# Cross attention and a routed feed-forward layer on one core: head-turns, running sums and the end of attention placed elsewhere

## The reference, cut to what matters

```python
q = l2norm(latents @ Wq) * q_scale            # latents = layer_norm(layernorm(x))
k, v = split(concat([ctx, latents]) @ Wkv)    # k = l2norm(k) * k_scale
sim = einsum('bhid,bhjd->bhij', q, k) * 8
sim = where(full_mask, sim, -max)
attn = softmax(sim)                            # over 64 + 1024 keys
out = einsum('bhij,bhjd->bhid', attn, v)
x = x + layer_norm(out @ Wo)
xf = layernorm(x)
x = x + shared_swiglu(xf) + top2_of_16_experts(xf)
```

## Time and profile before

| | |
|---|---|
| median of 3 runs | 820.85 us (819.99 to 821.29) |
| the profiled execution | 821.29 us, of which its span is 819.6 us |
| TensorE busy | 796.2 us (97%) |
| VectorE, ScalarE, GpSimd busy | 500.8, 342.8, 361.2 us |
| attention's eight pairs | from about 111 to 476 us |
| granted TensorE clock, mean | 0.996 |

### The profile page before, as it was taken

The page is one execution under the profiler, slowest core; times in us unless marked ns, Lnnn a source line. Parts: engine busy times, 40 slices in busy tenths (PEclk is TensorE's granted clock), DMA queues, the critical chain, the costliest instruction groups (busy, mean ns, idle before and its releaser), DMA issues.

```text
span 819.6 us, 13057 instructions
## 1 busy us (share of the span) xinstructions
PE 796.2 (97%) x4375; PEld 485.5 (59%) x4376; DVE 500.8 (61%) x918; ACT 342.8 (42%) x645; POOL 361.2 (44%) x259
## 2 busy tenths in 40 slices
PE   7999999999999999999999979999999999999997
PEld 4444455555554555455544446766557999999654
DVE  3888767778686878687787376647212334333254
ACT  3545465565655666565665311121111333333110
POOL 2100035868586785868588932301661000000374
PEclk9999999999999999999999989999999999999999
DMA  4014700000000000000020011591522222222243
GB/s 117 27 39 157 261 1 1 1 27 1 27 2 27 1 27 2 3 26 1 27 65 27 14 53 38 160 333 54 186 90 70 91 90 90 90 90 90 78 144 107
DMA packets 52373, 55.99 MB, mean 68 GB/s; under 512 B 8922, under 2 KB 47460, under 8 KB 52324
## 3 DMA queue, kind: packets, MB, share of 16 engines
q1 hardware_dynamic: 49236, 46.96, 18.0%
q0 software_dynamic: 3072, 8.39, 3.1%
q10 hardware_dynamic: 16, 0.00, 0.0%
HBM read 36.60 MB, written 18.67 MB: 67 GB/s over the span
## 4 chain that ended last, share of the span: by engine, by line
PE 88%; issue 4%; POOL 3%; ACT 2%; DVE 2%; DVEq 0%; DMA 0%; POOLq 0%; SPq 0%; ACTq 0%
PE bank L1109 14%; PE bank L925 12%; PE bank L950 11%; PE bank L1172 10%; PE bank L798 10%; PE bank L1124 7%; PE bank L884 6%; PE bank L1181 5%; PE bank L930 4%; PE bank L1016 2%; PE bank L868 2%; POOL acc L698 2%; PE bank L1162 1%; ACT prob L1288 1%; PE bank L945 1%
## 5 line engine op out<-in xcount | busy, mean ns | idle before, releaser
L1498 DVE TENSOR_REDUCE mx<-bank 128x1 f32<-128x512 f32 x256 | 164.4, 686 | 46.3 <-PE bank L884 45.1
L1288 ACT ACTIVATE prob<-bank,zero 128x512 f32<-128x512 f32 x256 | 161.0, 684 | 74.7 <-PE bank L930 72.2
L698 POOL TENSOR_TENSOR acc<-acc,prob 128x1024 f32<-128x1024 f32 (+1 forms) x72 | 179.3, 2491 | 10.3
L950 PE MATMUL bank<-prob,vn 128*64 128x512 f32 x512 | 121.1, 602 | 0.0
L1109 PE MATMUL bank<-xfT,w12s 128*128 128x512 f32 x256 | 117.6, 605 | 0.8 <-ACT xfT L1345 0.8
L760 POOL DMA_INDIRECT slot_result<-slot_results,posi x32 | 31.2, 973 | 160.1 <-DMA slot_results<-yo 148.2
L690 POOL TENSOR_TENSOR acc<-prob 128x1024 f32<-128x1024 f32 x16 | 41.1, 2566 | 119.8 <-ACT prob L1288 98.2
L1172 PE MATMUL bank<-xsT,w_slot 128*128 128x128 f32 x752 | 91.9, 275 | 1.0 <-ACT xsT L1379 1.0
L1172 PEld LDWEIGHTS bank<-xsT,w_slot 128*128 128x128 f32 x752 | 89.2, 192 | 6.0 <-ACT xsT L1379 1.6
L1109 PEld LDWEIGHTS bank<-xfT,w12s 128*128 128x128 f32 x256 | 49.5, 194 | 51.5 <-issue 50.2
L1369 ACT ACTIVATE hidden_units<-bank 128x512 f32<-128x512 f32 x32 | 19.1, 597 | 132.9 <-PE bank L1109 132.9
(11 more groups left out here) (172 smaller groups left out, 1123.5 us busy)
## 6 DMA issues: line engine op xcount, KB each, us to landing
w12r<-in_L_ffn_routed_w SPq DMA_DIRECT2D x32, 256.0 KB, 4.2
slot_rows<-zrow SPq DMA_DIRECT2D x47, 128.0 KB, 1.9
xsl<-slot_rows SPq DMA_DIRECT2D x47, 128.0 KB, 2.0
slot_results<-yo SPq DMA_DIRECT2D x47, 128.0 KB, 1.7
w3r<-in_L_ffn_routed_w SPq DMA_DIRECT2D x16, 256.0 KB, 3.5
rec<-row_sum_reciprocals SPq DMA_DIRECT2D x28, 128.0 KB, 2.9
xin<-in_x SPq DMA_DIRECT2D x16, 128.0 KB, 2.0
w12s<-in_L_ffn_shared_w SPq DMA_DIRECT2D x2, 1024.0 KB, 6.6
```

The source lines that it names most:

```text
L698: g.tensor_tensor(acc[rows, c, :, :], acc[rows, c, :, :], prob[rows, n % PROBS, :, :], ALU.add).then_inc(summed, 1)
L950: last = mm_(o_bank(i, c)[rows, :], vn[:, kt, b, (2 * j + h) * DH:(2 * j + h + 1) * DH], prob[:, n % PROBS, h, :], start=(s == 0), stop=(s ...
L1288: a(prob[rows, held % PROBS, h, :], bank[2 * (n % 2) + h][rows, :], ACT.Exp, bias=bias[rows, :])\
L1498: v.tensor_reduce(mx[:, h, t, c:c + 1], ring_bank(u)[:, :], AX.X, ALU.max).then_inc(ring_used, 1)
```

## The change

1. Turns go to the head of phases 1, 2 and 4 (K_LEFT; Q_LEFT; K_RIGHT and K_CTX), ahead of the rounds of that position. The rounds of phases 1 to 5 move by a position or so: phase 3 now has round 0 at its head, none ahead of the second slot, and rounds 2 and 4 behind.
2. VectorE's additions move: `add_two` of tiles 6 and 7 from the end of phase 2 to the end of phase 3, `add_both` from inside phase 3 to the head of phase 4, `add_two` of tiles 15 and 16 from the end of phase 5 to the end of the next pair's phase 0. `invert_sums` moves to the end of phase 2, `divide` to the ends of phases 3 and 5.
3. `total_pair` goes from behind phase 0 to phase 1, ahead of its value products.
4. GpSimd takes `tail` of the left half later (`ADDED`), and in the last pair earlier (`LAST_ADDED`), with the bias additions ahead of that pair.
5. In the last pair the left sum comes behind phase 3, `project_o(0)` behind phase 4, `project_o(1)` behind phase 5. The right sum goes through ScalarE, `spread`, a 128x8 inversion and DRAM.

```diff
-LEFT_SUMMED, SUMS = 8, 13
+LEFT_SUMMED, SUMS = 11, 13
+LAST_LEFT_SUMMED = 6
...
-    NEXT_TURNS = {(1, 3): (K_LEFT,), (3, 0): (Q_LEFT,), (3, 3): (K_RIGHT, K_CTX)}
-    OWN_ROUNDS = {0: ((), (8,), (9,), (10,)), 1: ((11,), (12,), (13,), ()), 2: ((14,), (15,), (RIGHT_MASKED,), ())}
-    NEXT_ROUNDS = {3: ((), (0,), (2,), ()), 4: ((4,), (6,), (1,), (3,)), 5: ((5,), (7,), (LEFT_MASKED,), ())}
+    NEXT_TURNS = {(1, 0): (K_LEFT,), (2, 0): (Q_LEFT,), (4, 0): (K_RIGHT, K_CTX)}
+    OWN_ROUNDS = {0: ((), (8,), (9,), (10,)), 1: ((), (11,), (12,), (13,)), 2: ((), (14,), (15,), (RIGHT_MASKED,))}
+    NEXT_ROUNDS = {3: ((0,), (), (2,), (4,)), 4: ((), (6,), (1,), (3,)), 5: ((5,), (), (7,), (LEFT_MASKED,))}
...
+            sp.wait_ge(sum_kept, PAIRS)
+            sp.wait_ge(rec_ready, PAIRS - 1)
+            for rows in (LOW, HIGH):
+                sp.dma_start(spread[rows, 0:LAST_COLS], rec[rows.start:rows.start + 1, 0, :]
+                             .rearrange("a (p c) -> a p c", c=LAST_COLS)).then_inc(sum_spread, 16)
+            sp.wait_ge(rec_ready, PAIRS)
+            sp.dma_start(rec_dram[1, 0:2 * QC].rearrange("(p c) -> p c", p=P), spread_rec[:, 0:LAST_COLS])\
+                .then_inc(rec_stored, 16)
...
             if i == PAIRS - 1:
-                pool.wait_ge(c_loaded, 48)
-                add_bias(0)
-                add_bias(1)
+                add_last(i, 0, LEFT_TAIL, LAST_LEFT_SUMMED)
             add_first(i, 1, BOTH + 1)
             add_more(i, 1, BOTH, HIGH)
-            add_last(i, 0, LEFT_TAIL, LEFT_SUMMED)
-            for s in range(BOTH + 3, BOTH + 7):
+            for s in range(BOTH + 3, BOTH + 6):
                 add_more(i, 1, s)
+            if i < PAIRS - 1:
+                add_last(i, 0, LEFT_TAIL, LEFT_SUMMED)
+            add_more(i, 1, BOTH + 6)
+            if i == PAIRS - 1:
+                deviations_c(0)
             add_last(i, 1, TAILS, SUMS)
...
+                if f == 1 and i:
+                    total_pair(i - 1)
                 for one in weighed:
                     weigh(*one)
-                if f == 0 and i:
-                    total_pair(i - 1)
-                if not more and f == 4:
+                if not more and f == 3:
                     total(NCH - 2)
-            if not more:
-                project_o(0)
+                if not more and f > 3:
+                    project_o(f - 4)
...
+                if f == 4 and more:
+                    v.drain()
+                    add_both(i)
                 for a in range(len(slots) + 1):
-                    if f == 1 and a == BATCH and i:
-                        invert_sums(i - 1)
-                    if f == 3 and a == BATCH:
-                        v.drain()
-                        add_both(i)
-                        if i:
-                            divide(2 * i - 2)
...
+                if f == 0 and i:
+                    add_two(i - 1, BOTH + 7, left_summed(i - 1))
                 if f == 2:
                     negate(1)
+                    if i:
+                        invert_sums(i - 1)
+                if f == 3:
+                    if more and i:
+                        divide(2 * i - 2)
                     add_two(i, 6, 0)
...
+                if f == 5 and more:
+                    negate(0)
+                    if i:
+                        divide(2 * i - 1)
```

More of the change, by code:

```diff
@@ L349, in build @@
             for a in range(len(slots) + 1):
+                for turn in place_turns(i, f, a):
+                    ring_put("turn", *turn)
                 for j, r in place_rounds(i, f, a):
                     ring_rounds(j, (r,))
-                for turn in place_turns(i, f, a):
-                    ring_put("turn", *turn)
+            if f == 1 and i:
+                ring_put("sums", i - 1)
             if BOTH in WEIGHED[f]:
                 ring_put("o", i)
-            if f == 0 and i:
-                ring_put("sums", i - 1)
-            if i == PAIRS - 1 and f == 4:
-                ring_put("sum", NCH - 2)
+    ring_put("sum", NCH - 2)
     ring_put("y", 0)
@@ L554, in _, with spread_last @@
         repeat_rec(PAIRS - 2)
+        def spread_last():
+            sp.wait_ge(sum_kept, PAIRS)
[6 more added lines that the diff above has]
+                .then_inc(rec_stored, 16)
+            sp.wait_ge(rec_stored, 16 * PAIRS)
+            for h, rows in enumerate((LOW, HIGH)):
+                sp.dma_start(rec[rows, 1, :], rec_dram[1:2, h * QC:(h + 1) * QC].to_broadcast([DH, QC]))\
+                    .then_inc(rec_loaded, 16)
         w3_rows = sw3[0].rearrange("(u p) d -> p u d", p=P)
@@ L706, in _ @@
         for i in range(PAIRS):
+            if i == PAIRS - 1:
+                pool.wait_ge(c_loaded, 48)
+                add_bias(0)
+                add_bias(1)
             if i:
@@ L737, in _ @@
         g.drain().then_inc(d_consts, 1)
-        for t in range(2, TQ):
+        for t in range(EARLY + 1, TQ):
             deviations_c(t)
@@ L1013, in project_o @@
                 pe.wait_ge(y_used, t)
+            if t == EARLY + 1:
+                pe.wait_ge(sum_kept, PAIRS)
             for c in range(B):
@@ L1326, in stage_b @@
                     keep_o(i - 1, 1)
+                if f == 2 and i:
                     keep_sums(i - 1)
@@ L1337, in _ @@
             stage_b(i)
+        u = ring_at[("sum", NCH - 1)]
+        act.wait_ge(ring_made, made_to(u))
+        act.wait_ge(o_ready, NCH - 1)
+        a(rec[:, 0, :], ring_bank(u)[:, :], ACT.Copy).then_inc(sum_kept, 1)
         def copy_xfT(t):
@@ L1558, in invert_sums, with invert_last @@
             v.reciprocal(spread_rec[:, :], spread[:, :]).then_inc(rec_ready, 1)
+        def invert_last():
+            dve.wait_ge(sum_spread, 64 * (PAIRS - 1) + 32)
+            dve.wait_ge(rec_stored, 16 * (PAIRS - 1))
+            v.reciprocal(spread_rec[:, 0:LAST_COLS], spread[:, 0:LAST_COLS]).then_inc(rec_ready, 1)
         sum_squares(NT - 1, 1, True, 2 * (NT - 1))
@@ L1652, in _ @@
         stage_c(0)
+        add_two(PAIRS - 1, BOTH + 7, LAST_LEFT_SUMMED)
         stage_c(1)
+        invert_last()
+        stage_c(EARLY)
         divide(NCH - 1)
         v.drain()
-        stage_c(EARLY)
         hid = 0
```

56 lines of the change are left out of this document (33 added, 23 removed).

## The result

The changed kernel takes 882.21 us (median of 4 runs, 881.05 to 884.88) where the kernel before takes 820.88 us beside it: ratio 1.075, 95% interval 1.073 to 1.0771. It is **slower by 61 us**; 888 us was predicted. The profiled execution has a span of 883.2 us, 63.6 us above the one before, where the sum said 67.6.

A forecast was written before the change was run, and what follows sets the result against it. With TensorE 97% busy, only its queue's order and small waits were taken to matter. Terms -5.4 + 7 + 2.1 + 48.2 + 21.7 - 6 = +67.6 us on 819.6 gave 887.2; forecast 888 us, first three cases 826 to 893.

The forecast's parts named there:

- The additions at the pair's head: Pair heads: moving `add_two` of tiles 15 and 16 removes a 0.9 us wait in six pairs, -5.4 us.
- The rounds: Phases 0 to 5: two rounds and two masked ones leave ScalarE's floor, +1.0 us a pair, +7 us.
- the sums inside phase 1: Phase 1: sums right behind round 13 wait 0.3 us for a bank still being reduced, +2.1 us over seven.
- The border: Phases 3 to 4: TensorE idles until K_RIGHT's split, 7.3 us in six pairs, 4.4 in pair 0, +48.2 us.
- The strict alternation: Border of phases 3 and 4: GpSimd and VectorE take turns on the shared port; likeliest case, 888 us, chance 0.42.
- the reciprocals: Border of phases 3 and 4: loaded for `divide` at +2.1 us, counted from round 4 at position 3 of phase 3.
- TensorE's clock: After each of seven border waits the granted clock falls to its lower level, 3.1 us lost each, +21.7 us.
- The end: Behind attention: 4.11 us idle before `xf`'s second turn and 3.1 us low clock go, new waits come, -6 us.
- the way over DRAM: Last sums' inversion, 6.2 us and some, lies beside the third projection and the first shared units.
- one turn kept: Rival, border: VectorE keeps the port for the instruction right behind, 4.95 us a pair, 854 to 875 us, chance 0.25.
- no collision: Border, lower end: VectorE never meets GpSimd, wait 0.9 us a pair, 826 us; in the rival of chance 0.15.

The follow-up runs named there:

- experiment 6: The kernel before with only the addition of tiles 15 and 16 moved behind the next pair's phase 0 head, joint sums a phase on: 816.92 us, ratio 0.9944.
- experiment 10: experiment 8 with `divide` one round up, directly behind `add_both`: 828.43 us, ratio 1.0093.
- experiment 5: experiment 1 with `add_both` also put back, ahead of the round at position 3 of phase 3: 837.81 us, ratio 1.0192.
- experiment 1: The changed kernel with `add_two` of tiles 6 and 7 back behind phase 2's negated maxima, except in the last pair: 864.7 us, ratio 1.0481.
- experiment 2: The changed kernel with GpSimd's right-half additions narrowed from 512 to 8 columns a head in all pairs but the last: 837.29 us in one run.
- experiment 3: The changed kernel with VectorE's two border additions narrowed from 512 to 8 columns a head in all pairs but the last: 850.19 us in one run.
- experiment 4: The changed kernel with the load of the fourth residual tile ahead of `spread_last` on SyncE's queue: 881.08 us, ratio 1.0678.
- experiment 8: experiment 5 with `invert_sums` ahead of phase 2's last slot instead of behind `negate(1)`: 840.88 us, ratio 1.0202.
- the joined version: The kernel before's phases, rounds and border additions, with the change's head addition, sums and end, and SyncE's order of experiment 4: 812.17 us, ratio 0.9879.

## Why the prediction came out as it did

The runs form a ladder, read from the first to the last turned maxima: kernel before 333.0 us, experiment 6 327.6, experiment 10 338.4, experiment 5 348.0, experiment 1 372.0, the change 392.3. They come from different chips; phases 0 to 2 take 23.4 us in all that have the changed tables (experiments 1, 5, 10 and the change), so this step can be read across them.

- **The additions at the pair's head, -5.4 us.** Right in place and size: 333.0 to 327.6 us is -5.4 us (experiment 6).
- **The rounds, and the sums inside phase 1, +7 and +2.1 us.** Nearly right: 327.6 to 338.4 us is 10.8 us, of which 2.5 us are the wait of 0.42 us left in six pairs; the other 8.3 us stand where 9.1 were taken. This step holds all of the placement of turns and rounds; which part of it is whose wasn't tried apart.
- **The border, +48.2 us.** Right in mechanism, and shown from both sides by experiments 2 and 3. The waits sum to 45.2 us: 4.04 us in pair 0, where 4.4 were taken, and some 6.85 us in the six others, where 7.3 were. The strict alternation held in all seven pairs; each turn costs what is left of GpSimd's instruction and then VectorE's own. That VectorE might keep the port once didn't happen at this border. One step of it held by a narrow margin: the reciprocals, taken at +2.1 us, landed up to +3.9 us, just ahead of the end of GpSimd's first instruction. A few tenths later, as in one pair of experiment 4, the order breaks and the wait is 5.17 us.
- **A link the prediction missed.** The division also holds ScalarE's copy, and through it `k_hi` (experiment 5). In the changed kernel this lies beside the longer wait: ScalarE's `k_hi` starts at 298.47 there, 6 us ahead of `k_lo`. It surfaces when the additions are gone, and cost experiments 5 and 8 their 9.6 and 9.0 us over experiment 10, one fall of the clock in each included.
- **TensorE's clock, +21.7 us.** The falls came, seven of them, but this term was sized too large. The change lies 53.9 us above experiment 10 (392.3 - 338.4), which has 0.42 us of wait left in six pairs; with 45.2 us of waits, 11.2 us are left (53.9 + 2.5 - 45.2) for all seven falls and anything else, 1.6 us each instead of 3.1. Pair by pair it is 0.9 to 2.2 us. The price was read from a stretch in which TensorE worked 6.05 of 6.83 us. Here the fall begins inside the wait itself: of 302.49 to 309.32, TensorE works only 4.05 us, and half of that is what a clock of 0.50 can cost, about 2 us.
- **The end, -6 us.** This step failed in sign. The wait of 4.11 us before the second turn of `xf` is gone, as said, though one of 3.20 us stands at a later turn, and from the last turned maxima to the end it is 380.0 us instead of 375.4, +4.6 us. The new waits for the two sums were 0.65 us (at 510.53) and 2.22 us, where 1 and 1.9 us were taken. A wait of 1.23 us that it didn't have stands before the projection at 518.03. What the prediction left out most is who stands behind SyncE's new work. In its queue, then GpSimd's and TensorE's timelines:

```profile
538.12 1.13 SPq L570 DMA_DIRECT2D spread<-rec  x2
541.39 0.33 SPq L573 DMA_DIRECT2D row_sum_reciprocals<-spread_rec  x1
542.85 1.10 SPq L577 DMA_DIRECT2D rec<-row_sum_reciprocals  x2
543.99 1.06 SPq L559 DMA_DIRECT2D xres<-in_x  x2
...
548.45 1.26 POOL L703 TENSOR_TENSOR xres<-xres,lno 128x512 f32<-128x512 f32 x1 [7.97 <-DMA xres<-in_x]
...
550.81 0.88 DVE L1696 SCALAR_TENSOR_TENSOR x<-yn,rs,xres 128x256 f32<-128x256 f32 x2 [7.53 <-POOL rs L668]
...
556.18 1.13 PE L1157 MATMUL bank<-w3s,hidden_units 128*128 128x256 f32 x4 [2.80 <-DVE hidden_units L1674]
...
569.56 0.69 PE L1094 MATMUL bank<-ident,xf 128*128 128x128 f32 x2 [3.20 <-DVE xf L1460]
```

  `spread_last` holds SyncE from 538.12 to 543.9, the load of the residual tiles goes out at 543.99, and GpSimd waits 7.97 us for it with the bias addition, behind which the deviations of the next tiles stand. VectorE gets them at 550.81, and TensorE loses 2.80 and then 3.20 us, the second with a fall of the clock at 568.70. The prediction put the way over DRAM beside the third projection and costed it at nothing, by its data alone; it named no instruction behind it on the queue. Experiment 4 shows this: with the load moved ahead, both waits go and the end takes 375.2 us, 4.8 us less, and that with the late wait of 2.67 us in it. In the joined version it takes 372.2 us, so of the 6 us that were predicted 3.2 us can be had.

The total came close by luck in this: two terms erred in opposite ways, the end by +10.6 us, and the clock by some -10 (11.2 instead of 21.7). The large term, 48.2 for 45.2 us, came out of its own mechanism. Two of the rivals' times don't follow from the prediction's own terms: one turn kept adds up to 852.7 us and not 854, and no collision to 825 us and not 826. Nothing hangs on either. The Trainium skill, in "SBUF — State Buffer", section "SBUF: two separate sides", has whichever instruction starts first take the shared port pair for its length; the rows above agree, each VectorE addition ending 1.08 us behind a GpSimd instruction that had begun ahead of it. In experiment 10 VectorE starts 0.36 us ahead and isn't slowed.

## What to carry to other kernels

Before moving VectorE work with two SBUF inputs into a gap, count how many such instructions in a row would meet a GpSimd that always has more: each pays the rest of a GpSimd instruction (some 2 us here), whatever its own size, and what matters is the instruction that stands behind them. The same work placed where GpSimd waits for data costs its own time, and 0.4 us of start decide between the two. For every step that is put in a queue, DMA issue included, write down what stands behind it there and who waits for that: five DMA issues that nothing needed yet cost 5 us here, since a load stood behind them.

## What was not expected of the hardware

- The length of a wait doesn't tell by itself whether the clock falls. It fell at every wait of 3.5 to 4.4 us at the border in experiment 1, and behind one of 2.18 us in experiment 4 (0.51 granted in the 3.40 us from 535.7). In experiment 3, with waits of 2.73 to 3.00 us in six pairs, it fell behind three of them and not behind the others. In experiment 5 it fell behind a wait of 1.61 us that ended at 422.05, and not behind the same wait in other pairs; the kernel before idled 1.74 us, and experiment 2 once 2.00 us, without a fall.
- The fall can begin while TensorE is still idle, and then costs less than its length says: 302.49 to 309.32 in the change with 4.05 us of work, 290.97 to 297.80 in experiment 1 with 5.13 us.
- Tiny VectorE instructions are held back as well, here one with a single tensor input. The negated maxima, 128x8, take 0.17 us in pair 0, where GpSimd does nothing. In the other 14 cases of the change they begin inside a GpSimd addition, take 0.8 to 2.2 us and end 0.03 us behind it. So they do in the joined version, where they take 0.4 to 0.7 us in all but one, since they begin later in that addition. Below are all of them in the change (shortest, median and longest, in ns) and one pair's:

```profile
L1547 DVE TENSOR_SCALAR zneg<-mm x16: 171/1360/2221, 108.5 to 501.1; 128x8 f32<-128x8 f32 x16
...
317.41 1.74 DVE L1547 TENSOR_SCALAR zneg<-mm 128x8 f32<-128x8 f32 x1
...
316.77 2.35 POOL L724 TENSOR_TENSOR acc<-acc,prob 128x1024 f32<-128x1024 f32 x1
```
